# A recommender tower on one core: the first couple leaves GpSimd's list of additions, and the second layer is summed output half by output half

## The reference, cut to what matters

```python
e = jnp.stack([tbl_0[ids[:, 0]], ..., tbl_39[ids[:, 39]]], axis=1)
viW = jnp.einsum('bpd,pde->bpe', e[:, i_idx, :], W)
z = jnp.einsum('bpe,bpe->bp', viW, e[:, j_idx, :])
h = jnp.concatenate([z, dense_ctx], axis=1)
h = jnp.maximum(h @ W_top1 + b_top1, 0.0)    # 796 -> 512
h = jnp.maximum(h @ W_top2 + b_top2, 0.0)    # 512 -> 256
y = h @ W_top3                               # 256 -> 1
```

## Time and profile before

| | us |
|---|---|
| median of 3 runs (lowest, highest) | 341.06 (340.83, 341.58) |
| the profiled execution, its own time | 341.38 |
| its span in the trace | 339.6 |
| TensorE busy in the span | 311.5 |
| VectorE busy | 250.1 |
| GpSimd busy | 233.4 |
| ScalarE busy | 218.9 |

### The profile page before, as it was taken

The page is one execution under the profiler, slowest core; times in us unless marked ns, Lnnn a source line. Parts: engine busy times, 40 slices in busy tenths (PEclk is TensorE's granted clock), DMA queues, the critical chain, the costliest instruction groups (busy, mean ns, idle before and its releaser), DMA issues.

```text
span 339.6 us, 5565 instructions
## 1 busy us (share of the span) xinstructions
PE 311.5 (92%) x1472; PEld 109.4 (32%) x1472; DVE 250.1 (74%) x252; ACT 218.9 (64%) x1696; POOL 233.4 (69%) x194
## 2 busy tenths in 40 slices
PE   0699879969999997599999999999999999999997
PEld 0133332323333332133333333233333332333442
DVE  2385868777989888098899899989999989930000
ACT  1001210297987979369797999989999999700032
POOL 6777777777777787878766799798898466900000
PEclk9999999999999999599999999999999999999999
DMA  5833434343334369141322322332212200000000
GB/s 160 243 120 85 121 90 117 92 113 94 101 77 121 91 190 281 31 99 49 104 59 86 90 70 73 84 94 70 59 60 66 62 1 0 3 0 2 0 0 0
DMA packets 17866, 27.67 MB, mean 81 GB/s; under 512 B 4901, under 2 KB 5029, under 8 KB 17834
## 3 DMA queue, kind: packets, MB, share of 16 engines
q1 hardware_dynamic: 12074, 21.00, 20.5%
q0 software_dynamic: 4608, 4.73, 6.7%
q10 hardware_dynamic: 1152, 1.57, 1.6%
HBM read 22.57 MB, written 0.00 MB: 66 GB/s over the span
## 4 chain that ended last, share of the span: by engine, by line
PE 50%; POOL 31%; issue 12%; DVE 5%; DMA 1%; ACT 0%; DVEq 0%
POOL rows L340 25%; PE ps_t L558 21%; PE ps_z L580 9%; PE ps_t L541 8%; PE ps_t L606 5%; POOL wide_rows L340 5%; DVE prod L466 4%; PE ps_t L641 2%; PE ps_e L606 2%; POOL prod L347 1%; PE ps_e L520 1%; DVE batched L480 1%; DMA ids_sb<-in_ids_t 1%; PE ps_t L647 1%; DVE z L487 0%
## 5 line engine op out<-in xcount | busy, mean ns | idle before, releaser
L384 ACT ACTIVATE batched<-batched 128x64 f32<-128x64 f32 x832 | 198.7, 244 | 6.4 <-DVE batched L480 6.4
L466 DVE TENSOR_TENSOR prod<-ps_t,E 128x1024 f32<-128x1024 f32 x148 | 170.9, 1217 | 21.1 <-PE ps_t L558 19.9
L384 ACT ACTIVATION_READ_ACCUMULATOR batched<-batched 128x1 f32 x832 | 158.5, 190 | 0.0
L558 PE MATMUL ps_t<-E,w_sb 64*128 64x512 f32 x592 | 145.4, 614 | 4.9 <-issue 2.6
L340 POOL DMA_INDIRECT rows<-in_tbl,ids_sb x128 | 121.8, 952 | 38.1 <-issue 38.0
L347 POOL TENSOR_TENSOR prod<-prod 128x1024 f32<-128x1024 f32 x40 | 93.5, 2368 | 19.7 <-DVE prod L466 19.6
L558 PEld LDWEIGHTS ps_t<-E,w_sb 64*128 64x128 f32 x592 | 51.0, 185 | 88.3 <-issue 58.1
L480 DVE TENSOR_TENSOR batched<-ps_t,wide_rows 128x1024 f32<-128x1024 f32 x52 | 60.0, 1217 | 15.4 <-PE ps_t L541 15.4
L580 PE MATMUL ps_z<-prod,quads 128*32 128x512 f32 x352 | 52.6, 611 | 6.0 <-POOL prod L347 6.0
L368 ACT ACTIVATE E<-ps_e 128x512 f32<-128x512 f32 x18 | 10.8, 598 | 65.2 <-PE ps_e L520 42.8
L541 PE MATMUL ps_t<-w_sb,E 64*128 64x512 f32 x208 | 49.1, 612 | 0.0
(11 more groups left out here) (41 smaller groups left out, 60.6 us busy)
## 6 DMA issues: line engine op xcount, KB each, us to landing
w_sb<-in_w_units SPq DMA_DIRECT2D x50, 256.0 KB, 2.8
E<-E SPq DMA_DIRECT2D x48, 64.0 KB, 2.0
rows<-in_tbl,ids_sb POOLq DMA_INDIRECT x128
w_sb<-in_w SPq DMA_DIRECT2D x7, 256.0 KB
E<-E ACTq DMA_DIRECT2D x24, 64.0 KB, 2.1
prod<-in_ids_by_field SPq DMA_DIRECT2D x2, 512.0 KB, 9.1
prod<-in_tbl SPq DMA_DIRECT2D x3, 312.5 KB
w_sb<-in_w SPq DMA_DIRECT2D x1, 512.0 KB
```

The costliest lines, as they stand in the source:

```text
L384: last = act.activation(products, products, ACT.Copy, accum_out=zt[:, b, at:at + 1])
L466: dve.tensor_tensor(prod[:, n % P_RING, s, :, :], ps_t[:, step % STEPS, :, :], multiplier, ALU.mult).then_inc(product_ready, 1)
L558: last = pe.matmul(ps_t[:, step % STEPS, j, :], w_sb[at:at + DIM, m % W_RING, col:col + P], E[at:at + DIM, slot_of(pairs_of(n)[s][j]), :], ...
```

## The change

Couple 10 is taken out of the list of couples whose halves GpSimd adds. GpSimd has 38 additions instead of 40, and `reduce_two(20)` runs over both halves of groups 20 and 21. In the second layer the loop over output halves m becomes the outer one: all four input blocks of half 0, then all four of half 1. The wait for the ReLU of each input block stays with half 0, and each half signals ScalarE when its own four blocks are in.

```diff
-ADDED_COUPLES = (10, 14, 15, 16, 18, 19, 20, 21, 23, 24, 25, 26, 27, 28, 30, 31, 32, 33, 34, 35)
+ADDED_COUPLES = (14, 15, 16, 18, 19, 20, 21, 23, 24, 25, 26, 27, 28, 30, 31, 32, 33, 34, 35)
...
-            for c in range(H1 // P):
-                pe.wait_ge(h1_ready, c + 1)
-                for m in range(H2 // P):
+            for m in range(H2 // P):
+                for c in range(H1 // P):
+                    if m == 0:
+                        pe.wait_ge(h1_ready, c + 1)
                     last = pe.matmul(h2_bank[m], w2_sb[:, c, m * P:(m + 1) * P], h1[:, c, :],
                                      start=(c == 0), stop=(c == H1 // P - 1))
-                    if c == H1 // P - 1:
-                        last.then_inc(h2_summed, 1)
+                last.then_inc(h2_summed, 1)
```

## The result

The changed kernel takes 335.35 us (median of 4 runs, 334.71 to 336.74), against 340.94 for the kernel before in the same comparison: a ratio of 0.984, 95% interval 0.982 to 0.986. It is faster by 5.6 us. The forecast was 334.0 with a range of 333.0 to 335.2, so the time lies 0.15 us above the range, and the gain is 1.5 us short of the 7.1 that the sum gave. The profiled execution took 335.7, with a span of 333.9. One run of the kernel before, at 527.52 us with a mean clock of 0.57, is left out of all that follows.

A forecast was written before the change was run, and what follows sets the result against it. TensorE sets the pace, except for one hole of 6.03 us before couple 10's reduction, made by GpSimd. -6.03 + 0.86 - 1.89 = -7.06, taken as 7.1 with part two at 0: 341.06 - 7.1 = 334.0 us, range 333.0 to 335.2.

The forecast's parts named there:

- the wait goes: -6.03 us: At couple 10's reduction TensorE no longer waits for GpSimd's addition of group 21: -6.03 us.
- the check that starts the walk at 133.98: Reduction starts at 133.98, after group 27's products; VectorE can follow, its batched multiply coming 7.05 us earlier, at 137.01.
- +0.86 for the longer reduction: Couple 10's reduction on TensorE grows from 8 records to 16: +0.86 us at full clock.
- -1.89 for the clock after the hole: Without TensorE's idle time before couple 10, reduction and batched unit run at full clock: -1.89 us.
- The walk behind the hole: After couple 10, VectorE, ScalarE and GpSimd can follow TensorE; the rest of the span moves about 7.1 us earlier.
- Part two: Second layer's new loop order: value 0, first ReLU 2.6 us earlier; bounds a gain of 0.10 or loss of 0.17 us.
- less comes back: After couple 10, VectorE and ScalarE carry their backlog on and TensorE meets them: 335.0 to 339 us; chance 0.10.
- The clock gives back more: Whole low-clock stretch, 136.96 to 143.8, counted at half its length, 3.42 us: time 332.5 us; chance 0.03.
- Rows that come late: TensorE stops again at the transposes of couple 13, its rows not yet there: 341.0 us; chance 0.02.
- another releaser of the hole: Something other than GpSimd holds couple 10's reduction until 140.0, so the wait stays: 341.9 us, slower; chance 0.03.

The follow-up runs named there:

- the useless work: Four transposes of field couple 7 made four times over: on the changed kernel 334.06 us, ratio 0.979; on the kernel before 341.26 us, ratio 1.000.
- part two alone: Kernel before with only the second layer's new loop order, couple 10 still in the list: 341.15 us, ratio 0.999.
- the delay: Four transposes of field couple 10 made eight times over: on the changed kernel 337.15 us, ratio 0.987; on the kernel before 339.76 us, ratio 0.995.
- the earlier copy: ScalarE copies field couple 7 ahead of the first two sums of batched unit 0: kernel before 341.51 us, changed kernel 333.49 us, ratio 0.977.
- the later gathers: Kernel before with gathers issued 12 groups ahead of use instead of 14, couple 10 still in the list: 334.64 us, ratio 0.979.
- the change once more: The same changed kernel run again for its spread, against the kernel before: 335.30 us, ratio 0.983.
- part one alone: Kernel before with only couple 10 taken out of the list, second layer in its old order: 334.30 us, ratio 0.978.

## Why the prediction was wrong, and where it was right

**The step that failed** is the first of the three terms, "the wait goes: -6.03 us", and the check that starts the walk at 133.98. Both took TensorE's arrival at couple 10 from one execution as if it were fixed. It is not: the products of groups 10 and 11 run at the full clock in some executions and partly at half of it in others, and TensorE arrives some 1.7 us later in the second kind. In the kernel before the wait measured 6.03 us, and 6.06 with the useless work; in part two alone, where the clock had fallen at 70 us, it measured 3.79. In the five profiles with the old list and the old order of gathers (the kernel before, part two alone, the useless work, the delay, the earlier copy) TensorE is done with group 27 anywhere between 132.95 and 137.09 us, and the reduction always starts between 139.78 and 140.47. So GpSimd set that time, and what the change gives back hangs on when TensorE arrives. The range allowed the runs a spread of 0.2 to 0.3 us; those of the new list lie between 333.20 and 337.55. All four rivals looked for trouble after 134 us; none asked what lay in front. The trace showed the place: 2.61 us of idle time on TensorE at 68 us, which my table of stretches, beginning at 75, left out. That an idle time brings the clock down I had read from the hole itself.

**The other terms stand.** Executions of the new list in which the clock stays up take 333.8 on average, and with the clock held up by useless work 334.06, against the 334.0 forecast. That fits the sum: +0.86 for the longer reduction (1.92 in place of 1.07 in the timelines; the later gathers, which do without it, come out 0.7 below the full change), -1.89 for the clock after the hole, which stayed up, and no loss further on.

**The walk behind the hole** was right to some 0.1 us relative to TensorE on VectorE and ScalarE. On GpSimd it was right where TensorE came as early as the forecast had it (145.14 and 4.82 for 145.2 and 4.9); in the profile of the change the agreement at 145.31 was luck. The rest of the span moved as one piece.

**Part two** was right: 0, with one ReLU earlier. Only the first matmul of layer three did not start 0.1 us earlier; it starts 6.96 us behind the second layer's start in both.

**The rivals.** The time lies in the band of "less comes back" (335.0 to 339), but not for its reason: no engine carried a backlog on, and VectorE was idle for 0.84 us where the forecast had 0.83. "The clock gives back more" is out at that place: held at full clock, the kernel gives 334.06 and not 332.5. The Trainium skill's price for throttled time ("TensorE: Matmul & The Clock Gate", Terms) gives an estimate of 3.42 us for that stretch. It overstates it here: the rows give 1.89, as 3.05 of the 6.84 us at the lower level lay in idle time. Rows that come late and another releaser of the hole did not occur.

## What to carry to other kernels

A wait on an engine with a fixed pace is also a buffer: it hides what varies in front of it, up to its own length. Before a wait is taken out at the size that one trace shows, look at what the waiting engine does from the start to there, above all at idle times behind which the clock may fall in some executions, and give the term the spread of several runs. Where TensorE must idle for some microseconds, useless work there can be worth more than it costs (334.06 for 335.30 us here). Moving what it waits for gave a little more (333.49), in another comparison.

## What the runs showed of the hardware that I had not expected

Idle times of nearly the same length on TensorE, at the same place, left the clock up or brought it down. At 68 us the clock stayed up after 2.61 us (kernel before), 2.65 (the change once more) and 2.75 (kernel before with the delay), and fell after 2.44 (part two alone), 2.67 (the changed kernel with the delay, and the later gathers) and 2.75 (the changed kernel, and part one alone). At 48 us it stayed up after 2.28 (the changed kernel) and 2.65 (the later gathers), and fell after 2.13 (part one alone). After the 1.40 and 1.45 us that the useless work left at 68 us, and the 0.73 that the earlier copy left, it stayed up in the profiles here. So a kernel can be slower by 1.7 us in one execution and not in the next with no difference in what it does.
